# Merge phase of an attention-and-experts kernel: router logits, exponential, table load, last choices and half of a weight's remainder moved

## What is computed

```
out_mem = silu(x_in @ w1'.T + b1') @ w2'.T + b2'
g1 = sigmoid(out_swa @ lin1.T)
g2 = sigmoid(out_mem @ lin2.T)
x1 = x + g1 * out_swa + g2 * out_mem
xn2 = (x1 - mean) / sqrt(var + eps)
probs = softmax(xn2 @ gate_w.T + gate_b)      # 8 experts, top 2, capacity 1.25
out = x1 + sum over the 2 choices of prob * (relu(xb @ W1[e] + b1[e]) @ W2[e] + b2[e])
```

## Time and profile before

| | |
|---|---|
| median of 3 runs | 2405.83 us |
| profiled execution, own time | 2407.89 us |
| its span | 2406.1 us |
| PE busy | 2341.6 us (97%), granted clock 0.989 |
| DVE busy | 1689.2 us (70%) |
| ACT busy | 1603.1 us (67%) |
| POOL busy | 1399.7 us (58%) |
| PE waits for m_hf, 1500 to 1872 us | 12 times |
| sigmoid table loads before L1978 | 14 of 1.283 us |

### The profile page before, as it was taken

The page is one execution under the profiler, slowest core; times in us unless marked ns, Lnnn a source line. Parts: engine busy times, 40 slices in busy tenths (PEclk is TensorE's granted clock), DMA queues, the critical chain, the costliest instruction groups (busy, mean ns, idle before and its releaser), DMA issues. The chain is left out here.

```text
span 2406.1 us, 39918 instructions
## 1 busy us (share of the span) xinstructions
PE 2341.6 (97%) x14802; PEld 2080.7 (86%) x14802; DVE 1689.2 (70%) x3661; ACT 1603.1 (67%) x2439; POOL 1399.7 (58%) x1002
## 2 busy tenths in 40 slices
PE   7999999799999999999999989999999999999998
PEld 6888888688888888888888978777777789999998
DVE  6787776466666666666666676777777757777776
ACT  4788888657777777777777646666766645554453
POOL 3565566556767776666767734666666553333433
PEclk9999999899999999999999999999999999999999
DMA  4222221532232332222233322332222165555551
GB/s 128 82 89 71 89 79 54 205 124 62 62 69 66 77 62 62 65 64 62 63 70 64 88 91 80 102 104 95 86 85 83 31 144 148 147 136 152 147 141 58
DMA packets 295393, 221.73 MB, mean 92 GB/s; under 512 B 189282, under 2 KB 262023, under 8 KB 295072
## 3 DMA queue, kind: packets, MB, share of 16 engines
q1 hardware_dynamic: 281376, 188.74, 29.2%
q0 software_dynamic: 13824, 30.44, 4.2%
HBM read 113.30 MB, written 72.12 MB: 77 GB/s over the span
## 5 line engine op out<-in xcount | busy, mean ns | idle before, releaser
L2653 ACT ACTIVATE e_hf<-e_ps_z,e_b 128x640 f32<-128x640 f32 x128 | 101.8, 795 | 214.1 <-PE e_ps_z L105 213.6
L2380 POOL TENSOR_TENSOR m_hl<-m_hf,m_hh 128x512 fp32r<-128x512 f32 x112 | 157.6, 1412 | 104.8 <-ACT m_hh L1983 103.4
L2780 POOL DMA_INDIRECT out<-e_ys,slot_token x80 | 83.2, 1040 | 217.9 <-DVE e_ys L2732 212.4
L105 PE MATMUL e_ps_y<-r_w_h,e_hl 128*128 128x256 f32 x640 | 180.3, 282 | 0.1
L105 PE MATMUL e_ps_y<-r_w_l,e_hh 128*128 128x256 f32 x640 | 178.8, 279 | 0.0
L105 PE MATMUL e_ps_y<-r_w_h,e_hh 128*128 128x256 f32 x640 | 178.7, 279 | 0.0
L1569 POOL TENSOR_TENSOR halves_l<-hT_full,halves_h 128x512 fp32r<-128x512 f32 x120 | 153.5, 1301 | 38.7 <-ACT halves_h L1229 38.7
L844 POOL DMA_INDIRECT xbuf_d<-xn,scatter_rows x128 | 147.3, 1151 | 41.8 <-issue 38.6
L701 POOL TENSOR_TENSOR prob<-prob,softmax_small 128x1024 f32<-128x1024 f32 x65 | 123.1, 1894 | 71.6 <-DVE softmax_small L634 71.6
L105 PE MATMUL e_ps_z<-slotsT_h,w_l 128*128 128x320 f32 x512 | 159.5, 311 | 0.5 <-DVE slotsT_l L2710 0.5
L105 PE MATMUL e_ps_z<-slotsT_l,w_h 128*128 128x320 f32 x512 | 159.4, 311 | 0.0
(11 more groups left out here) (342 smaller groups left out, 9034.9 us busy)
## 6 DMA issues: line engine op xcount, KB each, us to landing
shared_xT<-xT_d SPq DMA_DIRECT2D x64, 256.0 KB, 4.6
new_w1T<-in_W SPq DMA_DIRECT2D x16, 1024.0 KB, 5.1
new_w2T<-in_W SPq DMA_DIRECT2D x16, 1024.0 KB, 5.8
xbuf_d<-new_w1T SPq DMA_DIRECT2D x16, 650.0 KB, 8.0
shared_x<-in_x SPq DMA_DIRECT2D x16, 512.0 KB, 4.1
xn_d<-xn SPq DMA_DIRECT2D x32, 256.0 KB, 2.4
xT_d<-shared_xT SPq DMA_DIRECT2D x32, 256.0 KB, 2.6
oT_d<-shared_oT SPq DMA_DIRECT2D x32, 256.0 KB, 2.6
```

The lines of the kernel that those rows point to most:

```text
L105: i = e.matmul(out, a, b, start=first and not onto and n == 0, stop=last and n == len(terms) - 1, skip_group_check=onto)
L2380: e.tensor_tensor(hl[:, t, 0:N], hf[(HC * C + t) % NZ][:, 0:N], hh[:, t, 0:N], ALU.subtract).then_inc(*h_low(C, t))
L2653: e.activation(hf[(HC * i + t) % NHF][:].rearrange("p (s n) -> p s n", s=2), ps_z[t % 2][:, :, 0:HALF], ACTF.Relu, bias=b1[:, i % E, t:t + ...
L2780: e.indirect_dma_start(io["out"], bass.IndirectOffsetOnAxis(ap=token[i % 2][:, b:b + 1], axis=0), ys[:, b], None, bounds_check=NT - 1, oob ...
```

## The change

On PE the counts of chunk 14 (`dispatch`) go ahead of both parts of the last gate 2. On ACT `exponent(C-1)` moves ahead of `memory_out(C, 0)`, and a small sigmoid (`load_sigmoid`) stands between `split_x2(C-1)` and `memory_out(C, 1)` of every chunk from 1 on. On DVE `rest_xT(C+1)`, `router(C-1)` and `shift(C-1)` come right behind `norm_stats(C-1)`, ahead of `norm_apply(C-1)`; choices and weights of chunk 14 move into chunk 15, `dispatch(14)` ahead of the last second term. W1's low part is made in two column halves: the first at the very end of the phase's DVE queue, the second in the expert phase, with a new signal that `up(0, 4)` and `load_w1(1)` wait for. On POOL the scatter of chunk 14's first choices goes ahead of the two last roots.

```diff
--- before.py
+++ after.py
@@ -1957,8 +1957,8 @@
                 for _ in range(n):
                     e.matmul(ps_z[2][:], shared.keys[0][:, 0:P], shared.keys[0][:, 0:512], start=True, stop=True)
 
+            dispatch(NCH - 2)
             gate2_part(NCH - 1, 0)
-            dispatch(NCH - 2)
             gate2_part(NCH - 1, 1)
             keep_busy(2)
             residual(NCH - 1, 0)
@@ -2050,6 +2050,10 @@
                 act.wait_ge(*shifted.at(C, 1))
                 act.wait_ge(*weighed.at(C - 1, 2))
                 e.activation(pr[:, 0:SIZES[C]], below[:, 0:SIZES[C]], ACTF.Exp).then_inc(*exp_made(C))
+
+            def load_sigmoid():
+                act.wait_ge(*const_set.at(1))
+                e.activation(spare[:], neg_half[:, 0:1], ACTF.Sigmoid)
 
             for C in chunks:
                 tail = C >= 1
@@ -2084,6 +2088,8 @@
                     round_lin(1)
                 if C + 1 < NCH:
                     round_xT(C + 1)
+                if tail:
+                    exponent(C - 1)
                 memory_out(C, 0)
                 if C == NCH - 1:
                     for k in range(KC):
@@ -2094,11 +2100,8 @@
                     round_oT(C + 1)
                 if tail:
                     split_x2(C - 1, 0)
+                    load_sigmoid()
                 memory_out(C, 1)
-                if tail:
-                    exponent(C - 1)
-            act.wait_ge(*const_set.at(1))
-            e.activation(spare[:], neg_half[:, 0:1], ACTF.Sigmoid)
             for n in range(2):
                 gate2_part(NCH - 1, n)
             for k in range(2):
@@ -2338,29 +2341,25 @@
                     centre_gate()
                 if tail:
                     norm_stats(C - 1, 0)
-                    norm_apply(C - 1, 0)
                 if C + 1 < NCH:
                     rest_xT(C + 1)
+                if tail:
+                    router(C - 1)
+                    shift(C - 1)
+                    norm_apply(C - 1, 0)
                 rest_om(C, 0)
                 if C + 1 < NCH:
                     rest_oT(C + 1)
                 first_term(C)
                 add_x(C)
                 if C == NCH - 1:
-                    for k in range(KC):
-                        dve.wait_ge(*e_w1_high.at(k))
-                        e.tensor_tensor(w1l[:, k], g1[:, k], w1h[:, k], ALU.subtract)
+                    choose_experts(NCH - 2)
+                    weigh(NCH - 2)
                 rest_om(C, 1)
-                if tail:
-                    router(C - 1)
-                    shift(C - 1)
-            choose_experts(NCH - 2)
-            weigh(NCH - 2)
-            second_term(NCH - 1, 0)
-            merge(NCH - 1, 0)
             dispatch(NCH - 2)
-            second_term(NCH - 1, 1)
-            merge(NCH - 1, 1)
+            for n in range(2):
+                second_term(NCH - 1, n)
+                merge(NCH - 1, n)
             for n in range(2):
                 norm_stats(NCH - 1, n)
             norm_apply(NCH - 1, 0)
@@ -2370,6 +2369,8 @@
             norm_apply(NCH - 1, 1)
             weigh(NCH - 1)
             dispatch(NCH - 1)
+            dve.wait_ge(*e_w1_high.at(KC - 1))
+            e.tensor_tensor(w1l[:, :, 0:HID // 2], g1[:, :, 0:HID // 2], w1h[:, :, 0:HID // 2], ALU.subtract)
 
         def gpsimd(e):
             pool = Engine(e)
@@ -2407,9 +2408,9 @@
                 if C >= 2:
                     for k in range(TOPK):
                         scatter(C - 2, k)
+            scatter(NCH - 2, 0)
             for n in range(2):
                 root(NCH - 1, n)
-            scatter(NCH - 2, 0)
             scatter(NCH - 1, 0)
 
         def sync(e):
@@ -2530,6 +2531,7 @@
         w1_high, w2_high = signal("e_w1_high", halves_of[2:]), signal("e_w2_high", halves_of[2:])
         joined, xT_high, h_full = signal("e_joined", groups_of[len(groups[0]):]), signal("e_xT_high", groups_of), signal("e_h_full", ups)
 
+        first_w1_low = signal("e_first_w1_low", [0])
         cleared = signal("e_cleared", [0])
         by_act, by_dve = (0, 2, 4), (1, 3)
         act_joined, dve_joined = signal("e_act_joined", by_act), signal("e_dve_joined", by_dve)
@@ -2574,6 +2576,8 @@
             def up(i, t):
                 mc, out = slice(t * P, (t + 1) * P), ps_z[t % 2]
                 pe.wait_ge(*w1_low.at(i, KC - 1))
+                if (i, t) == (0, HC // 2):
+                    pe.wait_ge(*first_w1_low.at(0))
                 pe.wait_ge(*h_full.at(*before(i, t, 2)))
                 for s in range(2):
                     pe.wait_ge(*xT_low.at(*((0, 1) if (i, s) == (0, 0) else final_group(i))))
@@ -2735,6 +2739,7 @@
                 join_first(b)
             for n in range(len(groups[0])):
                 rest_first(n)
+            e.tensor_tensor(w1l[:, :, HID // 2:], s1[:, :, HID // 2:], w1h[:, :, HID // 2:], ALU.subtract).then_inc(*first_w1_low(0))
             slot_tokens(0)
             for k in range(2):
                 rest_w2(0, k)
@@ -2812,6 +2817,8 @@
 
             def load_w1(i):
                 sp.wait_ge(*w1_low.at(i - 1, KC - 1))
+                if i == 1:
+                    sp.wait_ge(*first_w1_low.at(0))
                 e.dma_start(s1[:], io["W1"][i % E].rearrange("(c p) n -> p c n", p=P)).then_inc(*w1_in(i))
 
             def load_w2(i):
```

## The result

| | before | changed |
|---|---|---|
| median, 22 runs each | 2405.60 us (2402.75 to 2409.27) | 2408.59 us (2406.07 to 2413.18) |
| ratio to before | | 1.0014, 95% interval 1.0008 to 1.0020 |
| profiled execution | 2407.89 us | 2408.02 us |

The change costs 3.0 us of 2405.6, 0.14%: less than the 0.2% that count as a difference here, though the interval leaves 1 out. What was forecast is 2408.5, within 0.2%.

What follows compares the result with a forecast made beforehand. PE, busy 97%, was taken as the bound, with a stall for m_hf. Per chunk -0.71 + 0.93 = +0.22, x14 = +3.1 us, tail -0.4, sum +2.7 on median 2405.83: 2408.5 us, 8-in-10 range 2396.5 to 2413.

Steps and rivals of the forecast that it cites:

- Old stall gone: PE's wait for VectorE's m_hf in the hidden layer goes away: 0.71 us a chunk at 14 boundaries, 9.9 us.
- steps 1 to 3: VectorE's rest_xT, with two SBUF inputs, blocks GpSimd's root, which ends at 1716.22 instead of 1715.30.
- steps 4, 5: ScalarE's chain from logits through exponential and sigmoid load: memory_out(C,0) 1.50 us later, memory_out(C,1) at 1722.98 instead of 1721.65.
- step 6: PE's second gate 2 product, waiting for keys_l, comes at 1725.35 instead of 1724.42: new stall 0.93 us a chunk.
- Tail -0.4: Last chunk's reordered dispatch, choices and scatters save 0.4 us; bounds +0.5 and -1.6.
- W1's other half 0: 1.21 us of VectorE work moved into the expert phase is covered by idle time: cost 0, within 0 to 1.2.
- First rival: GpSimd's root is not held up by rest_xT; new stall only 0.09 us, total 2396.7 us; chance 0.18.
- Second rival: GpSimd's delay reaches VectorE's merge, 0.3 us more a chunk, 2412.7 us; chance 0.18 together with the upper bounds.
- Third rival: Sigmoid's table load stays behind memory_out(C,1), so no stall at all: 2395.5 us; chance 0.02, counted with the free root.

Runs made afterwards that it cites:

- The filler: Changed kernel with rest_xT behind norm_apply and a same-size VectorE subtraction with one PSUM input in its old place: 2402.70 us, root 1.04 us.
- second profile: The changed kernel itself run and profiled again, nothing altered: 2407.16 us, ratio 1.0014 to the kernel before.
- the fast loop: Loop with early exponential, VectorE's new order and sigmoid's load behind memory_out(C,1): 2395.14 us with new tail, 2398.41 with old tail and W1.
- W1 in its old place: Changed kernel with sigmoid's load behind memory_out(C,1) and W1's low part back in the last chunk, new tail kept: 2399.58 us.
- a root made free in two ways: Changed kernel with rest_xT behind norm_apply, 2404.37 us; the same with a one-PSUM-input subtraction in rest_xT's old place, 2402.70 us.
- rest_xT between: Changed kernel with rest_xT moved behind shift, ahead of norm_apply: 2399.23 us, ratio 0.9980 to the kernel before.
- load behind: Changed kernel with the load for sigmoid back behind memory_out(C,1), exponential still early: 2395.14 us, 2396.83 in a repeat.

## Why the prediction held, point by point

- **Old stall gone, 0.71 a chunk.** Right: PE's wait for m_hf is gone from the list. But chunk 2 took 30.66 in the changed kernel, with neither stall: 13 stalls of gate 2, not 14. The chain of chunk 1 comes earlier: its root starts 8.12 us ahead of the next chunk (1469.38 - 1461.26), that of chunk 8 7.20 (1689.73 - 1682.53).
- **Root blocked by rest_xT (steps 1 to 3).** Right: 1682.53 to 1684.48, 1.95 long, where I had 1.96. The filler shows that it is the pair of SBUF inputs.
- **Logits to memory_out(C, 1) (steps 4, 5).** The logits start 0.14 behind the root instead of 0.03; from there 1.16 to the exponential, 0.14 to memory_out(C, 0), 5.43 to memory_out(C, 1): as worked out. The load for the exponential lies in idle time (1680.68).
- **New stall 0.93 (step 6).** Gate 2's second product is 1.01 later than before (3.98 against 2.97), the transposes 0.95 later than without any stall (11.99 against 11.04). Chunk 9 is 0.25 longer instead of 0.22; chunks 3 to 14 together are 3.35 longer (0.28 each, with chunk 10 in it), and chunk 2 is 0.68 shorter. That makes the 2.67 up to the start of chunk 15, whose last product is at +31.36 instead of +31.13: 2.90 in all, against 3.1. That these are so close is in part luck: the missing stall takes 0.90 off the forecast (-0.68 instead of +0.22), and the other 13 give 3.58 instead of some 2.9.
- **Tail -0.4, W1's other half 0.** The -0.4 is not borne out. Less the 0.23 by which chunk 15's own products end later, the stretch to the experts is 0.75 longer than before in the first profile and 0.02 in the second. The term that was too small is scatter(14, 0) ahead of the roots, reckoned at 4 x 1.28 = 5.1 us behind the last scatter of chunk 13. Timeline of GpSimd, second profile, the first two of its four instructions:

```profile
1918.83 0.97 POOL L844 DMA_INDIRECT xbuf_d<-xn,scatter_rows  x1 [0.51 <-issue]
1921.72 1.33 POOL L844 DMA_INDIRECT xbuf_d<-xn,scatter_rows  x1 [1.92 <-issue]
```

  With these pauses the four took 7.3 us (1918.32 to 1925.61), and the roots ended 44.62 behind the chunk's start instead of 44.13. A pause of 1.80 stands before the second of the four in the kernel before as well (ahead of 1925.46), and I had not counted it; what GpSimd does in it the profile doesn't show. In the expert phase VectorE casts the first e_hf at 1949.53, 1.08 after it is there (1948.45), so the cover of the earlier trace rows is used up and more; in the second profile the cast follows at once (1951.93; e_hf is there at 1951.90). PE shows no wait at that place. From the experts' first product to the end the eight profiles with the new place of W1 have 466.9 to 469.6 us, the four with the old one 467.5 to 469.7: no cost to be seen. What the -0.4 hid is that the pieces hang together: with the fast loop the tail gives 1.6 to 3.3 by the medians, and W1 in its old place takes it back.
- **First rival (free root, 2396.7).** The mechanism was excluded. Its stall of 0.09 is not what the steps give: with the root's end at 1715.30 instead of 1716.22 they give 0.93 - 0.92 = 0.01, which makes the price 1.1 us lower still. And the price was incomplete: with a root made free in two ways the time was 2404.4 and 2402.7, since the third chunk lost 7.1 us. With rest_xT between, where no scatter takes longer than 1.54 at that place, it comes out at 2399.2.
- **Second rival (delay reaches the merge).** Not in the changed kernel: merge is 2.27 us long and ends at 1701.45, 0.27 before the transposes. It decides in the two versions with a free root above, in chunk 3, and there costs far more than my 0.3 a chunk, by the clock.
- **Third rival (load does not move).** It moves. The price I gave for its place behind memory_out(C, 1), 2395.5, is what the version with the load behind took (2395.14, 2396.83).

The row of merge, timeline of VectorE, changed kernel:

```profile
1699.18 2.27 DVE L2157 TENSOR_TENSOR gate<-gate 128x1024 f32<-128x1024 f32 x1
```

## What to carry to other kernels

Work moved out of one hole has to be timed in the hole it is moved into: here the exponential's early place was good, and the load for sigmoid, put where ScalarE seemed idle, delayed the one piece that PE asks for next; left behind that piece, the kernel is 9 to 10 us faster than before instead of 3 slower. Before an instruction with two SBUF inputs is put beside a short GpSimd step on the critical chain, price that step at the instruction's remaining time on top. And moves at a phase's end are worth what they are worth together: here one of them left out took back what the others gained.

## What the runs showed that was not expected

- A GpSimd scatter can be kept out for several VectorE instructions with two SBUF inputs in a row, not just one: 4.42 and 4.41 us instead of 0.97, in chunk 2 alone, in both versions whose row was as above. In the next chunk the same row let it in at the first handover (1.85 us), and with rest_xT between, four such instructions in a row did no harm. What decides is open.
- After a single wait of 2.17 us PE was granted 0.50 until about 1524, which cost more than twice the wait itself.
- Gate 2's first half of chunk 15 is sometimes read late. Timeline of ScalarE, changed kernel:

```profile
1912.45 0.67 ACT L2011 ACTIVATE keys_h<-m_ps_o,new_b 128x512 fp32r<-128x512 f32 x1
1918.47 1.08 ACT L1995 ACTIVATE gate<-m_ps_z 128x512 f32<-128x512 f32 x2 [5.35 <-PE m_ps_z L105]
```

  The same kernel, second profile:

```profile
1918.38 0.60 ACT L1995 ACTIVATE gate<-m_ps_z 128x512 f32<-128x512 f32 x1 [2.63 <-PE m_ps_z L105]
1919.76 0.60 ACT L1995 ACTIVATE gate<-m_ps_z 128x512 f32<-128x512 f32 x1 [0.78 <-PE m_ps_z L105]
```

  Counted from the chunk's start the first read is at 38.67 in the one and 35.96 in the other, with PE at the same point in both (its first product at 34.16 and 34.17). The late form stands in three of the profiles with the new order of PE, and never where dispatch lies between the two halves. The stretch with it is 0.7 us longer here (59.26 against 58.53) and 1.7 in the version with the load behind (58.75 against 57.08); that all of this is its cost was not tried. Its cause was not tried.
